# A token mixer of attention and bilinear experts on one core: local heads' side work one piece per unit, the next chunk's first expert products among odd chunks' global heads, the first four masks in one group

## The reference

```
# attention: 16 heads of 16; heads 0..3 see all earlier tokens (global), heads 4..15 the last 64 (local)
scores = einsum(q, k) / 4; masked to -inf; w = softmax(scores); ctx = einsum(w, v); ctx @ w_out + b_out
# experts: Q = xn @ W_Q.T, K = xn @ W_K.T, and once more with both times W_inv.T
xV  = einsum('btd,kdr->btkr', Q_side, V)            # 8 experts of rank 64
cum = cumsum(einsum('btd,kdr->btkr', K_side, W), axis=1)
weights = softmax(gelu(Q_side @ router_w1.T + b1) @ router_w2.T + b2 + expert_bias)
out = einsum('btkr,kdr->btd', xV * cum * weights, U) + weights @ b;  out / n_valid
(fwd + alpha * inv) @ W_O.T
```

## Time and profile before

| | |
|---|---|
| median of 3 executions | 1487.94 us (1485.11 to 1491.22) |
| the profiled execution | 1491.34 us, span of its instructions 1489.6 us |
| PE busy | 1379.5 us, 93% of the span |
| DVE, ACT, POOL busy | 989.5, 776.1, 586.5 us |
| mean granted clock of PE | 0.989 |

### The profile page before, as it was taken

One profiled execution on the slowest core, in us unless ns is written; L12 is line 12 of the kernel. 1 busy time (PEld: TensorE's weight loads), 2 busy tenths in 40 slices (PEclk: granted clock), 3 DMA queues, 4 the chain that ended last, 5 costly groups with the idle time before them and its releaser, 6 DMA issues.

```text
span 1489.6 us, 35980 instructions
## 1 busy us (share of the span) xinstructions
PE 1379.5 (93%) x14481; PEld 1035.7 (70%) x14481; DVE 989.5 (66%) x2082; ACT 776.1 (52%) x1368; POOL 586.5 (39%) x663
## 2 busy tenths in 40 slices
PE   5978999999999999999999999999999999999996
PEld 4567685777758677586856778587775868667773
DVE  6667777567756777557875677566875578656661
ACT  2434537455464735645374554646356453755544
POOL 1025343453514444253433525144452534335341
PEclk9999999999999999999999999999999999999998
DMA  8430625326062541616353171624516153431610
GB/s 189 102 94 11 168 79 127 105 65 174 25 175 70 121 126 49 166 32 151 96 123 107 40 196 30 158 87 107 141 42 163 44 146 100 118 109 42 172 40 15
DMA packets 166614, 152.88 MB, mean 103 GB/s; under 512 B 37809, under 2 KB 149808, under 8 KB 166448
## 3 DMA queue, kind: packets, MB, share of 16 engines
q1 hardware_dynamic: 166448, 150.59, 38.8%
HBM read 108.57 MB, written 35.65 MB: 97 GB/s over the span
## 4 chain that ended last, share of the span: by engine, by line
PE 62%; DVE 15%; ACT 8%; issue 6%; DMA 4%; POOL 2%; SPq 1%; ACTq 0%; POOLq 0%; DVEq 0%
PE PS L676 30%; PE PS L787 11%; PE PS L821 4%; DVE rest L1193 3%; PE PS L880 3%; ACT HE L1063 3%; PE PS L807 3%; PE PS L909 3%; PE PS L898 2%; PE PS L963 2%; DMA weights_d<-weights_t 2%; DVE area L1198 2%; DVE area L1196 2%; ACT HE L1055 2%; ACT PS L1048 1%
## 5 line engine op out<-in xcount | busy, mean ns | idle before, releaser
L1504 POOL TENSOR_TENSOR PL<-prod,PH 128x512 fp32r<-128x512 f32 x128 | 164.7, 1287 | 201.3 <-ACT PH L1037 201.3
L676 PE MATMUL PS<-XH,WH 128*128 128x512 f32 x512 | 218.6, 427 | 21.7 <-ACT prod L1027 10.3
L1037 ACT ACTIVATE PH<-prod 128x512 fp32r<-128x512 f32 x128 | 80.8, 632 | 268.8 <-DVE prod L1305 252.8
L1499 POOL TENSOR_TENSOR prod<-prod,rest 128x512 f32<-128x512 f32 x96 | 124.8, 1303 | 242.9 <-DMA rest<-weights_d 166.6
L1229 DVE TENSOR_REDUCE block_peak<-PS 128x4 f32<-128x512 f32 x288 | 179.8, 685 | 48.0 <-PE PS L821 47.9
L676 PE MATMUL PS<-XH,WL 128*128 128x512 f32 x512 | 204.1, 399 | 0.0
L676 PE MATMUL PS<-XL,WH 128*128 128x512 f32 x512 | 203.6, 398 | 0.0
L1482 POOL TENSOR_SCALAR_AFFINE_SELECT HE<-HE 128x256 f32<-128x256 f32 x128 | 51.2, 406 | 364.2 <-ACT HE L1063 360.6
L1063 ACT ACTIVATE HE<-PS 128x512 f32<-128x512 f32 (+1 forms) x320 | 159.9, 553 | 33.5 <-PE PS L880 30.5
L1305 DVE TENSOR_TENSOR prod<-PS,prod 128x512 f32<-128x512 f32 x128 | 87.8, 686 | 97.3 <-PE PS L676 84.5
L676 PEld LDWEIGHTS PS<-XH,WH 128*128 128x128 f32 x512 | 97.1, 190 | 63.2 <-ACT prod L1027 16.8
(11 more groups left out here) (186 smaller groups left out, 3064.6 us busy)
## 6 DMA issues: line engine op xcount, KB each, us to landing
parts_d<-area SPq DMA_DIRECT2D x32, 768.0 KB, 5.0
area<-parts_d SPq DMA_DIRECT2D x128, 192.0 KB, 7.9
rest<-weights_d SPq DMA_DIRECT2D x192, 128.0 KB, 3.0
area<-parts_d SPq DMA_DIRECT2D x32, 576.0 KB, 7.8
tok<-in_L_attn_x_dram SPq DMA_DIRECT2D x16, 512.0 KB, 6.2
xt<-in_L_attn_x_dram SPq DMA_DIRECT2D x16, 512.0 KB, 4.1
wide<-weights_d SPq DMA_DIRECT2D x64, 128.0 KB, 3.0
out_dram<-xt SPq DMA_DIRECT2D x16, 512.0 KB, 3.8
```

The costliest lines, as they stand in the source:

```text
L676: ins = e.matmul(ps, a, b, start=first and k == 0, stop=last and k == n - 1, skip_group_check=True)
L1037: e.activation(PH[:, h, :], prod[:, j % 3, :], ACT.Copy).then_inc(phi)
L1499: e.tensor_tensor(prod[:, j % 3, :], prod[:, j % 3, :], wide[j % WIDE], ALU.mult).then_inc(weighed)
L1504: e.tensor_tensor(PL[:, j % 2, :], prod[:, j % 3, :], PH[:, j % 2, :].bitcast(F32), ALU.subtract).then_inc(plo)
```

## The change

Six edits:

1. Local heads: six side groups for six units (both `turn` and the last `mix`; `rows`; the four `parts`), where there were eight. `sums` stands behind the last of the `parts`. The running sums of both halves are made in the second `turn`. `parts` keeps its intermediate in `prod[0]` and `prod[2]` rather than in `rest`, so it no longer waits for `sums`.
2. DVE's part of `product` becomes a stage of its own, `times`.
3. Odd chunks with a next one: x of slices 1 and 2, c of 1 and 2, `times` 0 to 2, `weigh` 0 to 2, `product` 0 stand among the global heads' tiles. The chunk that follows starts with x of slice 3, `product` comes one slice and `mix` two slices later behind c than before.
4. The first four masks of a chunk (PE, stage `mask`) stand together ahead of the first four peaks.
5. `weights_d` is written by one DMA with all 128 rows of `weights_t`, where four DMAs wrote 8 rows each.
6. `wide` is read from it as two runs of 256 for each partition.

```diff
@@ -257,11 +263,21 @@
     def expert_groups(ch):
 
         order = []
+        if ch and ch % NC == 0:
+
+            x, c, mix = ([[(add, ch, j, part) for part in range(2)] for j in range(2 * KB)] for add in (add_x, add_c, add_mix))
+            order += [x[3] + [(add_weigh, ch, 3)], [(add_finish, ch - 1, 1), (add_product, ch, 1)]]
+            for j in range(3, 2 * KB):
+                order.append(c[j] + [(add_times, ch, j)])
+                order.append(([(add_open, ch)] if j == 3 else []) + mix[j - 3] + [(add_product, ch, j - 1)])
+                if j + 1 < 2 * KB:
+                    order.append(x[j + 1] + [(add_weigh, ch, j + 1)])
+            return order + [mix[5] + [(add_product, ch, 7)], mix[6]]
         for j in range(2 * KB):
             if j < 2 * KB - 1 and (j > 1 or not ch):
                 order.append([(add_x, ch, j + 1, part) for part in range(2)] + [(add_weigh, ch, j + 1)])
             order.append([(add_c, ch, j, part) for part in range(2)] if j else [])
-            order[-1].append((add_product, ch, j))
+            order[-1] += [(add_times, ch, j), (add_product, ch, j)]
...
@@ -312,8 +331,8 @@
         gpeaks = [[(add_gpeak, ch, t, j, peak_use())] for t in range(T) for j in range(c * T + t + 1)]
         masks = [[] for _ in order + gpeaks]
         for n, ((stage, *key),) in enumerate(order + gpeaks):
-            if stage is add_lpeak and n >= PEAKS:
-                masks[n].append((add_seed, key[-1], "lpeak", *key[:-1]))
+            if stage is add_lpeak:
+                masks[n].append((add_seed if n >= PEAKS else add_mask, key[-1], "lpeak", *key[:-1]))
...
@@ -324,7 +343,9 @@
             add_norm(1, order)
         blocks = range(0, len(order), PEAKS)
         joined = lambda groups, n: [stage for group in groups[n:n + PEAKS] for stage in group]
-        return [joined(order, n) + joined(masks, n + PEAKS) for n in blocks]
+        blocks = [joined(order, n) + joined(masks, n + PEAKS) for n in blocks]
+        blocks[0] = joined(masks, 0) + blocks[0]
+        return blocks
...
@@ -385,19 +406,23 @@
 
         experts, peaks = expert_groups(ch), peak_groups(ch)
         split = len(experts) - (0 if nxt else 4)
-        if ch:
+        if ch % NC:
             experts[1].append((add_finish, ch - 1, 1))
             experts[2], experts[3] = experts[3], experts[2]
-        run(experts[0] + peaks[0])
-        weave(experts[1:split], peaks[1:])
+        if ch and ch % NC == 0:
+            run(peaks[0])
+            weave(experts, peaks[1:])
+        else:
+            run(experts[0] + peaks[0])
+            weave(experts[1:split], peaks[1:])
         if ch:
             add_residual(ch)
 
         last_mix = [(add_mix, ch, 2 * KB - 1, part) for part in range(2)]
         if nxt:
-            side = [[(add_turn, ch + 1, 0)], last_mix, [(add_turn, ch + 1, 1)], [(add, "sums", ch + 1, 0), (add_rows, ch, 1)]]
-            side += [[(add_parts, ch + 1, 1, 0), (add, "sums", ch + 1, 1)]]
-            side += [[(add_parts, ch + 1, w, b)] for w, b in ((1, 1), (0, 0), (0, 1))]
+            side = [[(add_turn, ch + 1, 0), (add_turn, ch + 1, 1)] + last_mix, [(add_rows, ch, 1)]]
+            side += [[(add_parts, ch + 1, w, b)] for w in (1, 0) for b in range(DB)]
+            side[-1] += [(add, "sums", ch + 1, k) for k in range(DB)]
...
@@ -420,6 +445,35 @@
             run(first_x + order[0] + first_c)
             add("logits", ch + 1, uses=["bank7"])
             add("chigh", ch, 0)
+        if nxt and ch % NC:
+
+            blocks = len(order) // 2
+            scores, values = order[1::2], order[2::2]
+            x1, x2, c1, c2 = ([[(add, ch + 1, j, part)] for part in range(2)] for add, j in ((add_x, 1), (add_x, 2), (add_c, 1), (add_c, 2)))
+            if ch + 2 < CHUNKS:
+                add_norm(ch + 2, values[:9])
+            values[0] += [(add_gates, ch + 1), (add, "crest", ch, 0)] + x1[0]
+            values[1] += [(add_gate_parts, ch + 1)] + x1[1]
+            values[2] += x2[0]
+            values[3] += x2[1]
+            values[5].append((add_finish, ch, 0))
+            values[8].append((add_values, ch + 1, 0))
+            scores[8].append((add_weigh, ch + 1, 0))
+            values[9].append((add_times, ch + 1, 0))
+            scores[10].append((add_weigh, ch + 1, 1))
+            values[10] += c1[0] + c1[1]
+            values[11] += [(add_values, ch + 1, 1), (add_times, ch + 1, 1)]
+            scores[12] += [(add_weigh, ch + 1, 2), (add_product, ch + 1, 0)]
+            values[12] += c2[0] + c2[1]
+            for group in order[1:]:
+                run(group)
+            add("stacks", ch + 1, "global")
+            add("cturn", ch, 1)
+            add("chigh", ch, 1)
+            add_times(ch + 1, 2)
+            add("crest", ch, 1)
+            continue
...
@@ -1167,27 +1225,33 @@
                     i, c = 2 + k, ch % NC
                     q.wait_ge(xhi, DB * ch + k + 1)
                     e.tensor_tensor(XL[:, k, :], psum(i), XH[:, k, :].bitcast(F32), ALU.subtract).then_inc(xlo)
-                    if ch:
-                        q.wait_ge(part3, nth("parts", ch - 1, 0, k))
-                        q.wait_ge(weighed, nth("weigh", ch - 1, 6 + k))
-                    if ch == 1:
-                        q.wait_ge(bias_in, 16 * 15)
-                    if c:
-                        q.wait_ge(carried, DB * (ch // NC) + k + 1)
-                    e.tensor_tensor_scan(rest[:, k, :], psum(i), XH[:, k, :].bitcast(F32), carry[:, k:k + 1] if c else 0.0,
-                                         ALU.add, ALU.bypass).then_inc(bank_read[i])
-                    if c == 0:
-                        q.wait_ge(bank_read[i], use(f"bank{i}", *stage))
-                        e.tensor_copy(carry[:, k:k + 1], rest[:, k, C - 1:C]).then_inc(carried)
+
+                    for b in range(DB) if k == DB - 1 else ():
+                        i = 2 + b
+                        if ch:
+                            q.wait_ge(weighed, nth("weigh", ch - 1, 6 + b))
+                        if ch == 1:
+                            q.wait_ge(part3, nth("parts", 0, 0, b))
+                            q.wait_ge(bias_in, 16 * 15)
+                        if c:
+                            q.wait_ge(carried, DB * (ch // NC) + b + 1)
+                        e.tensor_tensor_scan(rest[:, b, :], psum(i), XH[:, b, :].bitcast(F32), carry[:, b:b + 1] if c else 0.0,
+                                             ALU.add, ALU.bypass).then_inc(bank_read[i])
+                        if c == 0:
+                            q.wait_ge(bank_read[i], use(f"bank{i}", "turn", ch, b))
+                            e.tensor_copy(carry[:, b:b + 1], rest[:, b, C - 1:C]).then_inc(carried)
 
                 elif kind == "parts":
                     ch, w, b = key
                     i = 2 + b
                     p1, p2, p3 = (parts[:, w, n if w else 2 - n, b, :] for n in range(3))
-                    left = rest[:, b, :]
+                    left = prod[:, (0, 2)[b], :] if ch else rest[:, b, :]
                     q.wait_ge(part1, nth(*stage))
-                    q.wait_ge(clo, DB * ch + b + 1)
-                    q.wait_ge(carried, DB * (ch // NC) + b + 1)
+                    if ch:
+                        q.wait_ge(plo, nth("product", ch - 1, (6, 5)[b]))
+                    else:
+                        q.wait_ge(clo, b + 1)
+                        q.wait_ge(carried, b + 1)
                     if w == 0:
                         q.wait_ge(part3, nth("parts", ch, 1, b))
                     e.scalar_tensor_tensor(out=left, in0=psum(i), scalar=(k_bias if w else q_bias)[:, b:b + 1], in1=p1,
...
-                    for w in range(2):
-                        for h in range(2):
-                            row = 32 * (2 * w + h)
-                            e.dma_start(weights_d[KE * w:KE * (w + 1), h * HALF:(h + 1) * HALF], weights_t[row:row + KE, :]).then_inc(weights_out, 16)
+                    e.dma_start(weights_d, weights_t[:, :]).then_inc(weights_out, 16)
...
+
+                    by_half = weights_d[2 * 32 * (j // KB):2 * 32 * (j // KB + 1), :].rearrange("(h e) t -> e h t", h=2)
                     for k in range(2):
-                        e.dma_start(wide[j % WIDE][R * k:R * (k + 1), :], weights_d[2 * j + k:2 * j + k + 1, :].to_broadcast([R, C])).then_inc(wide_in[j % WIDE], 16)
```

More of the change, by code:

```diff
@@ L172, in add_seed, with add_mask @@
         where[stage] = [int(bank[-1])]
+    def add_mask(bank, *stage):
+        add("mask", *stage)
+        plan.claim(stage, [bank])
+        where[stage] = [int(bank[-1])]
     def add_turn(ch, k):
@@ L277, in add_open, with add_times @@
         add("open", ch, uses=["bank0", "bank1"])
+    def add_times(ch, j):
+        add("times", ch, j)
     def add_product(ch, j):
@@ L422, in mixer_layer @@
             add("chigh", ch, 0)
+        if nxt and ch % NC:
[25 more added lines that the diff above has]
+            continue
+        if nxt:
             order = order[1:]
```

(19 more changed lines are left out.)

4 lines of the change are left out of this document (2 added, 2 removed).

## The result

| | before | after |
|---|---|---|
| median | 1486.53 us of 4 executions | 1498.03 us of 4 (1496.4 to 1501.21) |
| ratio, 95% interval | | 1.0064 (1.0039 to 1.0089) |
| profiled execution, its span | 1491.34, 1489.6 us | 1496.4, 1494.7 us |

The changed kernel is slower, by 11.5 us in the medians and 9.5 by the ratio.

A forecast was written before the change was run, and what follows sets the result against it. PE bound the kernel, its 110 us idle all there was to win. Eight even spans at +1.7 (+13.6), seven odd at -0.25 (-1.8) and 2 off gave +10: median 1487.94 becomes 1498, range 1465 to 1512.

The forecast's parts named there:

- Part 4: Local heads: POOL's sums hold DVE's last two parts; second `parts_out` 0.8 us later, x of slice 0 0.2 to 0.5 earlier.
- Rival A: Local heads: POOL's sums cost DVE's parts nothing (under 1 us), `parts_out` goes earlier; 1465 us, chance 0.28.
- Part 5: `weights_d` and `wide`: 96 KB more in the full queue costs 0.4 us; three issues less gain nothing.
- Part 1: Odd chunks' global heads, 7 spans: moved x1, x2, c1, c2 fill PE's waits, net 2.1 us less each.
- Part 2: Behind the moved products: PE stalls 2.6 us before peaks 5 to 8, in four pieces, the first about 1.4.
- Parts 1 and 2 cancel: Odd spans: the 2.1 us that the moved products save is offset by the 2.6 us stall before peaks 5 to 8.
- Part 3: First four masks in one group: saves 0.65 us of PE in odd spans, nothing in even ones.
- The wait for c of slice 1: Even spans: 1.24 us on average before, growing by 0.85 and 1.2 to 3.2.
- The clock: Falls to half clock cost 1.5 us each; charged 0.5 in an even span, 0.4 in an odd one.
- Rival C: Much slower: the clock falls in every even span and at every peak 5; 1513 us, chance 0.10.
- rival B: No change: the chain moves by under 0.5 us and no clock falls; 1486 us, chance 0.27.
- The signs: Right: odd spans near 91, even near 84.7, `parts_out` 22.3 us after start; wrong: `L1198` at 0.69, `wide` before 40.4.

The follow-up runs named there:

- second peaks later: The changed kernel with x of slice 3, `finish` and c of slice 3 issued ahead of peak 5 in even chunks: 1482.96 us, ratio 0.9966.
- Masks back: The changed kernel with each of the first four masks issued right ahead of its own peak again: 1499.19 us, ratio 1.0067.

## Why the prediction was right

The time came out where it was forecast, and the waits stand where the prediction put them: before peak 5, and before c of slice 1 behind a late `parts_out`. But the size is in part luck. I forecast some 3 us of length at full clock (13.6 and -1.8 less the clock in them, and the 2 taken off) and 6.8 of clock; the spans grew by 1.6 and 10.7.

**Part 4, local heads: right in kind, close in size.** Casts and subtractions of the last two parts lost 0.23, 0.98 and 0.99 us to POOL, together 2.2 (forecast 2.3). The second `parts_out` came 0.6 later for 0.8, x of slice 0 0.4 earlier in even spans for 0.2, 0.8 in odd ones for 0.5. The exclusive lock, cited from the Trainium skill, "SBUF — State Buffer", section "Who interferes with whom", fits: with the sums moved behind the parts the same instructions took 0.43 and 0.69. The same section exempts a VectorE instruction with at most one input in SBUF, outside the modes that use both ports; the trace agrees, `L1257`, with one input in PSUM, took 0.74 beside CH as without it. Rival A fell here: the sums cost the parts 2.2 us, not under 1.

**Part 5: sign right, a step wrong.** I wrote that three issues less gain nothing. They bring the first `wide` 0.34 forward; the shorter runs take 0.6 back at landing. Net 0.3 for 0.4, which the times are too coarse to show. Parts 4 and 5 together made even spans 0.64 longer at full clock, for 1.2.

**Part 1: mis-sized.** Waits worth 1.65 us were filled (2.67 to 1.02, and 0.13 for bank 4, which belongs to part 2), with new ones of 0.25 and 0.26 in the middle tiles, where I had charged 0.5; the named ones less that charge were 1.4. What I had added for restarts and short waits did not come: outside peaks 5 to 8 PE's own time did not fall. So the moved products saved 1.6, not 2.1, counted beside the stall; with the stall covered, the move is worth 0.7 (89.75 to 89.03, and 88.55 to 87.83).

**Part 2: right.** Peaks 5 to 8 were through 7.4 us after the first mask (forecast 7.2), in the four pieces that I had named: one wait of 1.32 and three of 0.18, 1.85 in all, the rest the slower peaks and 0.13 for bank 4 (0.25 forecast), 2.6 together. "Parts 1 and 2 cancel" (+0.5 without clock) came out as +0.98, by part 1.

**Part 3: right, and lost.** 0.68 measured for 0.65, but only without the stall. In the changed kernel it is nothing; I had added a saving in PE's time ahead of a wait that did not depend on it.

**The wait for c of slice 1: a row misread.** I took 1.24 us as its average before, from the 12.4 over 10 waits of the earlier trace rows. Three of the ten, 6.9 us, lie in the first chunk; in even spans it was 0.70. It grew by 1.8 us for the 2.05 that I added, but to 2.46 and not to 3.2.

**The clock: right in place, too small in size.** In these spans falls came in the waits for peak 5 and c of slice 1 or up to 2.9 us behind them, and nowhere else. I charged 0.4 in an odd span; the falls made the seven 5.4 us longer, 0.8 each. Even spans: 0.5 charged, 0.7 measured (the loss at half clock grew by 5.3 us in eight). Rival C, a fall at every such wait, did not hold: in the five profiles with the wait of 1.3 us before peak 5, 15 of 35 odd spans had a fall, and none of the 49 odd spans of the other seven profiles. The Trainium skill, "TensorE: Matmul & The Clock Gate", section "HAM oscillation", tells of a kernel that waits some 3 to 5 us for data in every round and whose clock falls each time. The four waits of over 3 us in these spans all had a fall; nearly all were shorter, and of those only some had one.

**The sum.** Forecast +13.6 in even spans, -1.8 in odd ones, -2; measured +10.3 and +2.0 in the profile, and 7.2 less outside the spans, most of that clock too. The runs put it more sharply: all but the moved products comes to nothing (ratio 0.9996: odd spans 1.5 shorter, even ones longer and with more falls), and moving them costs the 0.68% that is between that and the changed kernel. It is not the only edit of which this can be said: with the sums in another place the rest of the change is a gain of 0.6%. So what failed is the balance: an odd span became 0.3 us longer and not 0.25 shorter, by the clock, and the even-span chain was half as large as I had it at full clock. For all edits but the moved products, rival B, no change, would have been the right forecast.

**The signs.** Most came: odd spans at 90.7 without a fall, even ones at 84.8 with them (chunks 0 to 12), `parts_out` 22.0 us after the span's start, one wait over 1 us before peak 5, c of slice 1 waiting over 2. Two did not come cleanly. The last of the four subtractions took 0.69, a sign of being wrong: POOL held the cast ahead of it in its place (1.42). And the first `wide` of the span that I had named went out at 40.1, earlier than the 40.4 of before, another such sign; but 40.4 was the latest of the seven before, and their average grew, from 39.34 to 39.74.

What stays open: why a fall comes in one span and not in the next with the same wait. The twelve profiles together show that the length of the wait counts. Of the 96 waits for c of slice 1 (one in each even span) none of the 35 under 1.29 us had a fall, 18 of the 39 from there to 2.2 us did, and 19 of the 22 of 2.3 us and more. But length isn't all: waits of 2.72 and 2.84 us in the changed kernel had none, and second peaks later had seven falls with shorter waits on average (2.20) than the changed kernel's three (2.46). Masks back had none in odd spans with a wait of 0.92.

## What to carry to other kernels

Moving ready work into small waits uncovers what it had covered: look what reaches its wait first when the work is gone, and put other work there in the same edit. Ask for each helper instruction of GpSimd what VectorE instruction with two SBUF inputs, or cast, runs beside it; here, behind the last urgent one, the sums held nothing that anyone waited for. A saving of issue time ahead of a wait is worth nothing unless the wait moves with it. And before a total of waits is divided by their number, look where each of them lies.

## What the runs showed of the hardware

- A VectorE subtraction or cast begun beside GpSimd's CL ended 0.55 and 0.29 us after CL did, in 1.67 and 1.42 us for 0.69 and 0.43; GpSimd's CH, begun beside the subtraction, took 1.07 for 0.60.
- A load of 128 KB from DRAM took 3.6 us to land in runs of 1 KB and 3.0 in runs of 2 KB.
- A fall of the granted clock to 0.50 lasted 3.41 us or twice that in these spans. In or behind the wait for c of slice 1 it came in none of 35 spans with a wait under 1.29 us, in 18 of 39 with one of 1.29 to 2.2, and in 19 of 22 with one of 2.3 to 3.56.
- VectorE's casts and subtractions beside GpSimd's masks (0.66 to 0.72 us each) took 0.68 and 1.01 us, for 0.43 and 0.69 with nothing beside them.
